# Routing of a mixture-of-experts layer: integer indices compared as they are, picks seen kept per row group, slots summed straight into the records

## The chip, the core and the metric

The kernel runs on one core of one Trainium2 chip, in one launch. The time is device microseconds (us) of that core; three runs of the kernel before took 697.89, 700.32 and 699.39 us, median 699.39. The engines named below are TensorE (PE; its weight loads are PEld), VectorE (DVE), ScalarE (ACT), GpSimd (POOL) and SyncE (SP, which here only issues DMAs).

## The reference, cut to what matters

Tokens are rows of x, 2 x 2048 of them, 256 wide. An RWKV attention layer with a layer norm gives x1; then eight experts with top-2 routing and a second layer norm follow.

```python
x = layernorm(x + attention(x))                 # k, v, r projections, WKV scan over time, Wo
logits = einsum('bsd,de->bse', x, Wg) + bg      # 8 experts
scores, idx = top_k(logits, 2); scores = softmax(scores)
comb = (one_hot(idx, 8) * scores[..., None]).sum(axis=1)
h = einsum('td,edf->etf', tokens, W1) + b1      # 256 -> 1024, per expert
a = where(even expert, gelu(h), silu(h))
y = einsum('etf,efd->etd', a, W2) + b2          # 1024 -> 256
x = layernorm(x + einsum('te,etd->td', comb, y))
```

## The kernel before, in words

The work has two phases. Phase A goes over time in NCH = 8 chunks of TC = 256 steps of both batches, so that a chunk has N = 512 tokens, held as J = 4 row groups of P = 128 tokens (one token to a partition). Phase B goes over blocks of BLK = 256 tokens of one expert each, some 35 of them.

Every engine has its own program, and the order within it is written out by hand; semaphores tie them together. In phase A each engine works through steps i, and one step holds pieces of several chunks: on VectorE, step i is `stabilise(i)` (scan over k, tiles `o_all`, `nd`), `divide(i-1)` (tile `newton`), `place(i-3)`, `accumulate(i)` (the two long scans `q_all`, `p_all`), `numerator(i)`, the residual and the statistics of i-1, `choose(i-2)`, and `lower_halves(i+2)` (tile `xl`, the low part of the transposed input of a later chunk, for which ScalarE first makes `xh`). In the last steps chunk 5 is placed at the end of step 7, and chunks 6 and 7 are chosen and placed one after the other.

The routing of a chunk c is in these pieces:

- `score_rows` (TensorE) puts the 4 x 8 logits of each token into `lg_ps`.
- `choose` (VectorE) takes the maxima `m8` and their indices `i8` (uint32), casts the indices to float (`idxf`, L1265), compares them with 0..7 into the one-hot `hot` [4 groups, 2 picks, 8 experts] (L1267), and adds the two picks into `picks` (bf16, L1270). Semaphore `route` counts each of these.
- `rank_picks` (TensorE) works out how many tokens ahead of each one, in earlier partitions, earlier row groups and earlier chunks, chose each expert: five matmuls of at most 32 columns into `rank_ps`; the last (L803) multiplies `seen`, the sum over earlier chunks per partition and expert, [128, 8].
- `place` (VectorE) makes the softmax weights (L1329 to L1334), then `rank` (adds the start of each expert's region in DRAM, L1342), `newly` (picks of this chunk, summed over the row groups, L1343), `spread` (`hot` times `rank`, L1345), `seen` += `newly` (L1347), `slot_f` (sum of `spread` over experts, L1349), its integer copy `slot_i` (L1351) and its copy into the record (L1352). Semaphore `slots` counts them, and most of them wait for the one before.
- `send_records` (POOL) waits for all seven counts and then issues eight indirect DMAs, which scatter the chunk's 261-number records (x1, token number, two slots, two weights) into the expert regions (`records_dram`, L614). After them POOL computes the mean and spread of the next chunk (`spread_of`, tiles `var_e` to `shift`), from which ScalarE normalises x1.

Phase B's start hangs on the routing's end. SP loads two blocks early (`recs`), once chunks 0 to 4 (those below KNOWN = 5) are scattered; the scatter of chunk 5 waits for that load. After the last chunk is ranked, TensorE waits for `seen` (the fourth count of `slots`), counts all picks with one matmul (L859), and then begins the first expert product `hT_ps` (L871). VectorE makes the table of blocks from the counts. `idle_products` (L680) are matmuls whose result nobody reads.

Of the kernel before, what the change touches and what calls it, by code (L numbers as in the profile page):

```python
# [23 lines left out]
ALU = mybir.AluOpType  # L24
# [8 lines left out]
P = 128  # L33
# [50 lines left out]
def build(nc, x, decay, first, mix_k, mix_v, mix_r, wkT, wvT, wrT, woT, w1, b1, w2, b2, wgT, bg, out):  # L84
# [40 lines left out]
    with ExitStack() as ctx:  # L125
        def sb(name, shape, dt=F32, where=ctx):
            return where.enter_context(nc.sbuf_tensor(name, shape, dt))
# [78 lines left out]
        odds = sb("odds", [P, J], F32, phase_a)  # L206
        both = sb("both", [P, J], F32, phase_a)
        i8 = sb("i8", [P, J, 8], U32, phase_a)
        idxf = sb("idxf", [P, J, 2], F32, phase_a)
        hot = sb("hot", [P, J, 2, E], F32, phase_a)  # L210
        seen = sb("seen", [P, E], BF16, phase_a)
        newly = sb("newly", [P, E], F32, phase_a)
        picks = sb("picks", [P, J, E], BF16, phase_a)
        rank = sb("rank", [P, J, E], F32, phase_a)
        spread = sb("spread", [P, J, 2, E], F32, phase_a)
        slot_f = sb("slot_f", [P, J, 2], F32, phase_a)
        slot_i = [sb(f"slot_i{n}", [P, J * 2], I32, phase_a) for n in range(RECS)]
        const_rows = sb("const_rows", [5 * CC, P], F32, phase_a)
        b1_rows = sb("b1_rows", [E * FC, P], F32, phase_a)
# [100 lines left out]
        c_bn, c_mv, c_var, c_rstd, c_res = (sem(n) for n in ("c_bn", "c_mv", "c_var", "c_rstd", "c_res"))  # L320

        REC_DMAS = 2 * J * 16
        ROUTE1, ROUTE2 = 2 * J + 3, 7

        def chunks(body):

# [347 lines left out]
        def _(pe):  # L674
# [107 lines left out]
            def turn_early(n):  # L782
# [7 lines left out]
                        ins = pe.transpose(xT2_ps[:, cc, h * P:(h + 1) * P], recs[n][:, h, cc * P:(cc + 1) * P], ident[:])  # L790
                ins.then_inc(tx_done, 1)

            def rank_picks(c):
                if c.number == 0:
                    pe.wait_ge(halves_made, 1)
                pe.wait_ge(route, c.upto(ROUTE1))
                if c.number == KNOWN:
                    pe.matmul(early_ps, ones_h[:], seen[:], start=True, stop=True).then_inc(known, 1)
                pe.matmul(rank_ps, before_h[:], picks[:], start=True, stop=False)
                for j in range(J - 1):  # L800
                    pe.matmul(rank_ps[:, j + 1:J, :], ones_h[:], picks[:, j:j + 1, :].broadcast_to([P, J - 1 - j, E]),
                              start=False, stop=False)
                pe.matmul(rank_ps, ones_h[:], seen[:].unsqueeze(1).broadcast_to([P, J, E]), start=False, stop=True).then_inc(rank_done, 1)  # L803

            def step(i):
                if i.number == -2:
# [9 lines left out]
                else:  # L816
# [38 lines left out]
                    if routed.exists:  # L855
                        rank_picks(routed)
                        if routed.number == NCH - 1:
                            pe.wait_ge(slots, routed.upto(ROUTE2, 4))
                            pe.matmul(cnt_ps, ones_h[:], seen[:], start=True, stop=True).then_inc(cnt_done, 1)  # L859

            chunks(step)

# [274 lines left out]
        def _(dve):  # L1137
# [114 lines left out]
            def choose(c):  # L1252

                dve.wait_ge(lg_done, c.upto(1))
                take_wait(dve)
                for j in range(J):
                    dve.max(m8[:, j, :], lg_ps[:, j, :]).then_inc(route, 1)
                dve.wait_ge(route, c.upto(ROUTE1, J))
                take_wait(dve)
                for j in range(J):  # L1260
                    dve.max_index(i8[:, j, :], m8[:, j, :], lg_ps[:, j, :]).then_inc(route, 1)
                after(dve, weighed, (c - 1).upto(1))
                dve.tensor_tensor(gap[:], m8[:, :, 1], m8[:, :, 0], ALU.subtract).then_inc(gap_done, 1)
                dve.wait_ge(route, c.upto(ROUTE1, 2 * J))
                dve.tensor_copy(idxf[:], i8[:, :, 0:2]).then_inc(route, 1)  # L1265
                dve.wait_ge(route, c.upto(ROUTE1, 1 + 2 * J))
                dve.tensor_tensor(hot[:], expert_no[:].unsqueeze(1).unsqueeze(1).broadcast_to([P, J, 2, E]),  # L1267
                                  idxf[:].unsqueeze(3).broadcast_to([P, J, 2, E]), ALU.is_equal).then_inc(route, 1)
                dve.wait_ge(route, c.upto(ROUTE1, 2 + 2 * J))
                dve.tensor_tensor(picks[:], hot[:, :, 0, :], hot[:, :, 1, :], ALU.add).then_inc(route, 1)  # L1270

            def accumulate(i):
# [52 lines left out]
            def place(c):  # L1325
# [14 lines left out]
                    dve.wait_ge(known, 2)  # L1340
                    dve.tensor_tensor(rest_no[:], region_no[:], done_f[:], ALU.add).then_inc(known, 1)
                dve.tensor_tensor(rank[:], rank_ps, region_no[:].unsqueeze(1).broadcast_to([P, J, E]), ALU.add).then_inc(slots, 1)  # L1342
                dve.tensor_reduce(newly[:], picks[:].rearrange("p j e -> p e j"), AX.X, ALU.add).then_inc(slots, 1)  # L1343
                dve.wait_ge(slots, c.upto(ROUTE2, 2))
                dve.tensor_tensor(spread[:], hot[:], rank[:].unsqueeze(2).broadcast_to([P, J, 2, E]), ALU.mult).then_inc(slots, 1)  # L1345
                dve.wait_ge(slots, c.upto(ROUTE2, 3))
                dve.tensor_tensor(seen[:], seen[:], newly[:], ALU.add).then_inc(slots, 1)  # L1347
                dve.wait_ge(slots, c.upto(ROUTE2, 4))
                dve.tensor_reduce(slot_f[:], spread[:], AX.X, ALU.add).then_inc(slots, 1)  # L1349
                dve.wait_ge(slots, c.upto(ROUTE2, 5))  # L1350
                dve.tensor_copy(slot_i[c.number % RECS][:].rearrange("p (j k) -> p j k", j=J), slot_f[:]).then_inc(slots, 1)  # L1351
                dve.tensor_copy(rec[c.number % RECS][:, :, C + 1:C + 3], slot_f[:]).then_inc(slots, 1)  # L1352

            def residual_0(c):
                add_residual(c, 0)
# [153 lines left out]
```

## Time and profile before

| | |
|---|---|
| median of three runs | 699.39 us |
| the profiled execution | 698.79 us, its span 696.8 us |
| PE busy | 630.9 us, 91% |
| DVE busy | 464.1 us, 67%, 1075 instructions |
| ACT busy | 377.9 us, 54% |
| POOL busy | 333.2 us, 48% |
| mean granted TensorE clock | 0.952 |

The shares are means over both phases. In phase B, from 300 us on, PE is busy all the time and DVE a little over half of it; in phase A the two are close to each other, as the rows below show. A span starts with the first instruction and ends with the last; the profiled execution took 1.99 us more than its span.

### The profile page before, as it was taken

How to read it: one execution, taken by the hardware profiler on the slowest of the kernel's cores; microseconds unless marked ns; L12 is line 12 of the kernel's file. 1: busy time of each engine (PE TensorE's matmuls, PEld its weight loads, DVE VectorE, ACT ScalarE, POOL GpSimd, SP SyncE). 2: the span in 40 equal slices, each digit the busy share in tenths (PEclk: the TensorE clock that was granted, in tenths of full speed). 3: DMA queues.
4: the chain of work that ended last, by engine and by line, in shares of the span. 5: the costliest groups of instructions: out<-in, count | busy, mean ns of one | idle time of the engine just before them, and what ended most of it. 6: DMA issues, size and time to landing. Idle time of an engine off the chain costs nothing.

```text
span 696.8 us, 14651 instructions
## 1 busy us (share of the span) xinstructions
PE 630.9 (91%) x4525; PEld 581.3 (83%) x4525; DVE 464.1 (67%) x1075; ACT 377.9 (54%) x690; POOL 333.2 (48%) x322
## 2 busy tenths in 40 slices
PE   8999999999977788999999999999999999999800
PEld 5787887878854578999999999999999999999700
DVE  4879999999998566556556565565565465545334
ACT  3566686585764133645464646466464646464317
POOL 6111037536546768239356384356394275222325
PEclk9999999999989779999999999999999999999955
DMA  8500222321324745532534425325317313231376
GB/s 254 157 32 0 91 91 70 132 83 55 107 86 154 232 148 151 162 60 63 144 48 146 71 42 160 60 49 144 72 24 183 47 42 47 48 48 15 36 226 276
DMA packets 53309, 70.61 MB, mean 101 GB/s; under 512 B 5482, under 2 KB 46900, under 8 KB 53076
## 3 DMA queue, kind: packets, MB, share of 16 engines
q1 hardware_dynamic: 31012, 43.24, 18.8%
q0 software_dynamic: 13216, 17.09, 13.4%
q10 hardware_dynamic: 8976, 8.82, 4.5%
q8 instruction: 73, 1.20, 0.7%
q14 instruction: 32, 0.26, 0.1%
HBM read 40.86 MB, written 29.06 MB: 100 GB/s over the span
## 4 chain that ended last, share of the span: by engine, by line
PE 64%; DVE 16%; issue 8%; ACT 4%; DMA 3%; POOL 2%; SPq 0%; DVEq 0%; ACTq 0%; POOLq 0%
PE hT_ps L871 27%; PE y_ps L880 26%; PE vr_ps L708 3%; PE k_ps L708 2%; PE xT_ps L889 2%; ACT zz L1133 2%; DVE o_all L1221 2%; POOL records_dram L614 2%; DMA zz<-x_dram 1%; DVE newton L1244 1%; DVE newton L1249 1%; DVE stats L1319 1%; DVE newton L1242 1%; DMA recs<-records_dram 1%; DVE num L1311 1%
## 5 line engine op out<-in xcount | busy, mean ns | idle before, releaser
L871 PE MATMUL hT_ps<-xTh,wx 128*128 128x256 f32 x1120 | 207.5, 283 | 2.6 <-DVE aTl L1191 1.3
L652 POOL DMA_INDIRECT x_dram<-y_sb,dest x70 | 108.5, 1550 | 195.3 <-DVE y_sb L1208 128.1
L880 PE MATMUL y_ps<-wx,aTh 128*128 128x256 f32 x1088 | 191.1, 279 | 3.0 <-DVE y_sb L1208 3.0
L871 PEld LDWEIGHTS hT_ps<-xTh,wx 128*128 128x128 f32 x1120 | 174.8, 189 | 3.3 <-DVE aTl L1191 2.4
L1191 DVE TENSOR_TENSOR aTl<-hT_ps,aTh 128x512 fp32r<-128x512 f32 x140 | 93.3, 688 | 121.7 <-ACT aTh L1094 121.7
L880 PEld LDWEIGHTS y_ps<-wx,aTh 128*128 128x128 f32 x1088 | 165.5, 189 | 3.4 <-issue 3.4
L871 PE MATMUL hT_ps<-xTl,wx 128*128 128x256 f32 x560 | 156.9, 280 | 0.0
L880 PE MATMUL y_ps<-wx,aTl 128*128 128x256 f32 x544 | 151.7, 279 | 0.0
L1088 ACT ACT_TABLE_LOAD x33 | 42.3, 1283 | 162.5 <-PE hT_ps L871 160.8
L1088 ACT ACTIVATE hT_ps<-hT_ps,b_c 128x256 f32<-128x256 f32 x280 | 113.5, 468 | 22.8 <-PE hT_ps L871 21.2
L614 POOL DMA_INDIRECT records_dram<-rec,slot_i x64 | 76.7, 1198 | 67.6 <-DVE rec L1352 35.9
L871 PEld LDWEIGHTS hT_ps<-xTl,wx 128*128 128x128 f32 x560 | 106.1, 189 | 0.0
L880 PEld LDWEIGHTS y_ps<-wx,aTl 128*128 128x128 f32 x544 | 102.2, 188 | 0.0
L708 PE MATMUL vr_ps<-xh,wq 128*128 128x512 f32 x256 | 86.7, 411 | 0.0
L1094 ACT ACTIVATE aTh<-hT_ps 128x512 fp32r<-128x512 f32 x140 | 84.3, 649 | 0.0
L558 POOL TENSOR_TENSOR wx<-staging,wx 128x512 fp32r<-128x512 f32 x56 | 70.3, 1293 | 0.6
L708 PEld LDWEIGHTS vr_ps<-xh,wq 128*128 128x128 f32 x256 | 49.7, 194 | 11.8 <-ACT v L975 0.3
L1206 DVE TENSOR_TENSOR y_ps<-y_ps,b_b 128x256 f32<-128x256 f32 x70 | 30.1, 430 | 43.9 <-DVE weight L1187 18.9
L708 PE MATMUL vr_ps<-xl,wq 128*128 128x512 f32 x128 | 51.9, 405 | 0.0
L708 PE MATMUL k_ps<-xh,wq 128*128 128x512 f32 x128 | 42.2, 401 | 5.2 <-DVE nd L1228 4.2
L1208 DVE TENSOR_SCALAR y_sb<-y_ps,weight 128x256 f32<-128x256 f32 x70 | 33.9, 484 | 2.5
L708 PEld LDWEIGHTS k_ps<-xh,wq 128*128 128x128 f32 x128 | 24.2, 189 | 11.9 <-issue 6.3
(203 smaller groups left out, 853.5 us busy)
## 6 DMA issues: line engine op xcount, KB each, us to landing
staging<-in_L_ffn_W SPq DMA_DIRECT2D x16, 1024.0 KB
recs<-records_dram ACTq DMA_DIRECT2D x33, 261.0 KB, 3.0
xin<-in_L_attn_x SPq DMA_DIRECT2D x16, 256.0 KB, 4.3
xres<-in_L_attn_x SPq DMA_DIRECT2D x16, 256.0 KB, 3.1
x_dram<-rec SPq DMA_DIRECT2D x16, 256.0 KB, 3.4
zz<-x_dram SPq DMA_DIRECT2D x8, 512.0 KB, 9.2
out<-zz SPq DMA_DIRECT2D x8, 512.0 KB, 3.5
records_dram<-pad_rec SPq DMA_DIRECT2D x8, 261.0 KB, 2.9
```

What stands on the lines that cost most here:

```text
L558: pool.tensor_tensor(wx[:, e % 2, 1, at], raw[:, at], wx[:, e % 2, 0, at].bitcast(F32), ALU.subtract).then_inc(weights_ready if n == LOWER ...
L614: pool.indirect_dma_start(xs, bass.IndirectOffsetOnAxis(ap=slot_i[at][:, n:n + 1], axis=0), rec[at][:, j, :], None, bounds_check=DUMMY - 1 ...
L652: pool.indirect_dma_start(sums, bass.IndirectOffsetOnAxis(ap=dest[t.slot][:, h:h + 1], axis=0), y_sb[t.slot][:, h, :], None, bounds_check= ...
L708: ins = pe.matmul(out_ps.rearrange("p (b t) -> p b t", b=B), wq[:, mat, now, part, cc, oc * P:(oc + 1) * P], xpart[c.slot][:, cc, :, now:n ...
L871: ins = pe.matmul(hT_ps[b][:, f, :], wx[:, s, part, off:off + P], xpart[t.slot % 2][:, cc, :], start=k == 0, stop=k == len(terms) - 1)
L880: ins = pe.matmul(y_ps[h], apart[t.slot % 2][:, fc, h * P:(h + 1) * P], wx[:, s, part, off:off + C], start=k == 0, stop=k == len(terms) - 1)
L889: ins = pe.transpose(xT2_ps[:, cc, h * P:(h + 1) * P], recs[u.slot][:, h, cc * P:(cc + 1) * P], ident[:])
L1088: act.activation(hT_ps[b][:, f, :], hT_ps[b][:, f, :], func, bias=b1_c[:, bass.ds(expert * FC + (2 * b + f), 1)]).then_inc(act_done, 1)
L1094: act.activation(aTh[u.slot % 2][:, 2 * b - 2:2 * b, :], hT_ps[b - 1][:], ACT.Copy).then_inc(aTh_done, 1)
L1191: dve.tensor_tensor(aTl[u.slot % 2][:, 2 * b:2 * b + 2, :], hT_ps[b][:], aTh[u.slot % 2][:, 2 * b:2 * b + 2, :].bitcast(F32), ALU.subtract ...
L1206: dve.tensor_tensor(y_ps[h], y_ps[h], b2_b[:, bass.ds(expert * C, C)], ALU.add).then_inc(bias_added, 1)
L1208: dve.tensor_scalar(y_sb[u.slot][:, h, :], y_ps[h], weight[u.slot][:, h:h + 1], None, ALU.mult).then_inc(y_done, 1)
```

## The change

Three buffers go (`idxf`, `newly`, `slot_f`). `hot` compares the uint32 indices directly. `seen` has one row per row group, [128, 4, 8], so that the picks are added to it elementwise, with no sum over the groups; TensorE does that sum, with four matmuls into the same accumulator where there was one. The slots are summed straight into the record, and `slot_i` is cast from there.

```diff
-        seen = sb("seen", [P, E], BF16, phase_a)
+        seen = sb("seen", [P, J, E], BF16, phase_a)
-        ROUTE1, ROUTE2 = 2 * J + 3, 7
+        ROUTE1, ROUTE2 = 2 * J + 2, 5
 # TensorE
+            def count(out_ps):
+                for j in range(J):
+                    ins = pe.matmul(out_ps, ones_h[:], seen[:, j, :], start=j == 0, stop=j == J - 1)
+                return ins
 # rank_picks
-                pe.matmul(rank_ps, ones_h[:], seen[:].unsqueeze(1).broadcast_to([P, J, E]), start=False, stop=True).then_inc(rank_done, 1)
+                for j in range(J):
+                    ins = pe.matmul(rank_ps, ones_h[:], seen[:, j:j + 1, :].broadcast_to([P, J, E]), start=False, stop=j == J - 1)
+                ins.then_inc(rank_done, 1)
 # after the last chunk (and for chunk KNOWN, into early_ps, in the same way)
-                            pe.wait_ge(slots, routed.upto(ROUTE2, 4))
-                            pe.matmul(cnt_ps, ones_h[:], seen[:], start=True, stop=True).then_inc(cnt_done, 1)
+                            pe.wait_ge(slots, routed.upto(ROUTE2, 2))
+                            count(cnt_ps).then_inc(cnt_done, 1)
 # VectorE, choose
-                dve.tensor_copy(idxf[:], i8[:, :, 0:2]).then_inc(route, 1)
-                dve.wait_ge(route, c.upto(ROUTE1, 1 + 2 * J))
                 dve.tensor_tensor(hot[:], expert_no[:].unsqueeze(1).unsqueeze(1).broadcast_to([P, J, 2, E]),
-                                  idxf[:].unsqueeze(3).broadcast_to([P, J, 2, E]), ALU.is_equal).then_inc(route, 1)
+                                  i8[:, :, 0:2].unsqueeze(3).broadcast_to([P, J, 2, E]), ALU.is_equal).then_inc(route, 1)
 # VectorE, place
                 dve.tensor_tensor(rank[:], rank_ps, region_no[:].unsqueeze(1).broadcast_to([P, J, E]), ALU.add).then_inc(slots, 1)
-                dve.tensor_reduce(newly[:], picks[:].rearrange("p j e -> p e j"), AX.X, ALU.add).then_inc(slots, 1)
-                dve.wait_ge(slots, c.upto(ROUTE2, 2))
+                dve.tensor_tensor(seen[:], seen[:], picks[:], ALU.add).then_inc(slots, 1)
+                dve.wait_ge(slots, c.upto(ROUTE2, 1))
                 dve.tensor_tensor(spread[:], hot[:], rank[:].unsqueeze(2).broadcast_to([P, J, 2, E]), ALU.mult).then_inc(slots, 1)
                 dve.wait_ge(slots, c.upto(ROUTE2, 3))
-                dve.tensor_tensor(seen[:], seen[:], newly[:], ALU.add).then_inc(slots, 1)
+                dve.tensor_reduce(rec[at][:, :, C + 1:C + 3], spread[:], AX.X, ALU.add).then_inc(slots, 1)
                 dve.wait_ge(slots, c.upto(ROUTE2, 4))
-                dve.tensor_reduce(slot_f[:], spread[:], AX.X, ALU.add).then_inc(slots, 1)
-                dve.wait_ge(slots, c.upto(ROUTE2, 5))
-                dve.tensor_copy(slot_i[c.number % RECS][:].rearrange("p (j k) -> p j k", j=J), slot_f[:]).then_inc(slots, 1)
-                dve.tensor_copy(rec[c.number % RECS][:, :, C + 1:C + 3], slot_f[:]).then_inc(slots, 1)
+                dve.tensor_copy(slot_i[at][:].rearrange("p (j k) -> p j k", j=J), rec[at][:, :, C + 1:C + 3]).then_inc(slots, 1)
```

On VectorE, in the first step that places a chunk, these rows stand before, from the last product of `divide` to the first copy of `accumulate` (the three rows between are the softmax weights):

```order
L1249 SCALAR_TENSOR_TENSOR newton<-newton,num 128x2x256 x2
L1329 TENSOR_SCALAR both<-odds 128x4
L1332 RECIPROCAL rec<-both 128x4
L1334 TENSOR_TENSOR rec<-odds,rec 128x4
L1342 TENSOR_TENSOR rank<-small_ps,region_no 128x32
L1343 TENSOR_REDUCE newly<-picks 128x8
L1345 TENSOR_TENSOR spread<-hot,rank 128x64
L1347 TENSOR_TENSOR seen<-seen,newly 128x8
L1349 TENSOR_REDUCE slot_f<-spread 128x8
L1351 CAST slot_i<-slot_f 128x8
L1352 COPY rec<-slot_f 128x4x2
L1279 COPY B<-q_all 128x4
```

And now, on the same engine at the same place:

```order
L1253 SCALAR_TENSOR_TENSOR newton<-newton,num 128x2x256 x2
L1331 TENSOR_SCALAR both<-odds 128x4
L1334 RECIPROCAL rec<-both 128x4
L1336 TENSOR_TENSOR rec<-odds,rec 128x4
L1344 TENSOR_TENSOR rank<-small_ps,region_no 128x32
L1345 TENSOR_TENSOR seen<-seen,picks 128x32
L1347 TENSOR_TENSOR spread<-hot,rank 128x64
L1349 TENSOR_REDUCE rec<-spread 128x4x2
L1351 CAST slot_i<-rec 128x8
L1281 COPY B<-q_all 128x4
```

Seven rows behind the weights have become five: the sum over row groups and the copy into the record are gone, and `seen`, with 32 elements instead of 8, stands ahead of `spread`.

On TensorE these rows stand before at the end of phase A, from the last idle products to the first expert product:

```order
L680 MATMUL k_ps<-ones_h 128x512 x6
L799 MATMUL small_ps<-picks,before_h 128x32
L801 MATMUL small_ps<-picks,ones_h 128x24
L801 MATMUL small_ps<-picks,ones_h 128x16
L801 MATMUL small_ps<-picks,ones_h 128x8
L803 MATMUL small_ps<-seen,ones_h 128x32
L859 MATMUL small_ps<-seen,ones_h 128x8
L871 MATMUL hT_ps<-xTh,wx 128x256
```

And now:

```order
L677 MATMUL k_ps<-ones_h 128x512 x6
L801 MATMUL small_ps<-picks,before_h 128x32
L803 MATMUL small_ps<-picks,ones_h 128x24
L803 MATMUL small_ps<-picks,ones_h 128x16
L803 MATMUL small_ps<-picks,ones_h 128x8
L806 MATMUL small_ps<-seen,ones_h 128x32 x4
L792 MATMUL small_ps<-seen,ones_h 128x8 x4
L875 MATMUL hT_ps<-xTh,wx 128x256
```

The matmuls on `seen` are four where there was one, in the ranking and in the count; nothing else on TensorE has another place.

## Rows read from the trace of the kernel before

**Rows 1.** Windows: stretch, its length, busy us (x instructions) per engine, PEclk, DMA.
```profile
120.00:150.00 30.00, 27.75 (x140) 22.86 (x141) 29.16 (x64) 21.18 (x32) 13.91 (x16) 1.00 0.35 116
166.00:168.00 2.00, 2.00 (x8) 1.71 (x7) 1.68 (x20) 1.31 (x4) 1.54 (x4) 0.50 0.19 67
250.00:254.00 4.00, 4.00 (x19) 4.00 (x20) 3.56 (x16) 0.81 (x2) 2.15 (x3) 0.51 0.32 104
```
**Rows 2.** Timeline of PE: start, us, line, operation, count, idle before it and releaser.
```profile
145.24 0.22 PE L801 MATMUL small_ps<-picks,ones_h 128*128 128x24 bf16 x3
145.32 0.18 PE L803 MATMUL small_ps<-seen,ones_h 128*128 128x32 bf16 x1
146.96 0.47 PE L708 MATMUL k_ps<-xh,wq 128*128 128x512 f32 x1 [1.47 <-DVE nd L1228]
```
**Rows 3.** Chain that ended last, in order of time: start, us, what.
```profile
201.08 1.29 DVE newton L1249 x2
...
219.66 3.20 DMA recs<-records_dram
...
234.47 1.05 POOL rstd L591
...
249.97 9.08 PE hT_ps L871 x60
```
**Rows 4.** Timeline of DVE, `choose` in the step from 120 us.
```profile
141.46 0.17 DVE L1265 CAST idxf<-i 128x8 f32<-128x8 uint32 x1
141.67 0.23 DVE L1267 TENSOR_TENSOR hot<-expert_no,idxf 128x64 f32<-128x64 f32 x1
141.93 0.19 DVE L1270 TENSOR_TENSOR picks<-hot 128x32 bf16<-128x32 f32 x1
```
**Rows 5.** Timeline of DVE, `place` in the same step.
```profile
125.43 0.18 DVE L1342 TENSOR_TENSOR rank<-small_ps,region_no 128x32 f32<-128x32 f32 x1
125.53 0.20 DVE L1343 TENSOR_REDUCE newly<-picks 128x8 f32<-128x32 bf16 x1
125.76 0.22 DVE L1345 TENSOR_TENSOR spread<-hot,rank 128x64 f32<-128x64 f32 x1
126.02 0.17 DVE L1347 TENSOR_TENSOR seen<-seen,newly 128x8 bf16<-128x8 bf16 x1
126.22 0.22 DVE L1349 TENSOR_REDUCE slot_f<-spread 128x8 f32<-128x64 f32 x1
126.47 0.17 DVE L1351 CAST slot_i<-slot_f 128x8 int32<-128x8 f32 x1
126.56 0.16 DVE L1352 COPY rec<-slot_f 128x8 f32<-128x8 f32 x1
126.63 0.16 DVE L1279 COPY B<-q_all 128x4 f32<-128x4 f32 x1
```
**Rows 6.** Timeline of DVE: first row of `lower_halves` in two steps.
```profile
89.65 0.17 DVE L1296 CAST xl<-xl 128x4 fp32r<-128x4 f32 x1
...
168.24 0.17 DVE L1296 CAST xl<-xl 128x4 fp32r<-128x4 f32 x1
```
**Rows 7.** Timeline of ACT: the `xh` for which those rows wait.
```profile
88.54 1.07 ACT L1019 ACTIVATE xh<-xT_ps 128x512 fp32r<-128x512 f32 x2
...
166.81 1.07 ACT L1019 ACTIVATE xh<-xT_ps 128x512 fp32r<-128x512 f32 x2
```
**Rows 8.** Timeline of POOL: last scatter of chunk 3 and what follows it.
```profile
191.53 0.97 POOL L614 DMA_INDIRECT records_dram<-rec,slot_i  x1 [0.30 <-issue]
192.88 0.20 POOL L588 TENSOR_TENSOR var_e<-mv,eps_b 128x4 f32<-128x4 f32 x1 [0.38 <-issue]
```
**Rows 9.** Timeline of DVE: the last chunk's `place`.
```profile
248.94 0.19 DVE L1342 TENSOR_TENSOR rank<-small_ps,region_no 128x32 f32<-128x32 f32 x1 [0.57 <-PE small_ps L803]
...
249.54 0.17 DVE L1347 TENSOR_TENSOR seen<-seen,newly 128x8 bf16<-128x8 bf16 x1
```
**Rows 10.** Timeline of PE: the count of all picks, ahead of the first expert product.
```profile
249.76 0.19 PE L859 MATMUL small_ps<-seen,ones_h 128*128 128x8 bf16 x1 [1.36 <-DVE seen L1347]
```

More of the change, by code:

```diff
@@ L208, in build @@
         i8 = sb("i8", [P, J, 8], U32, phase_a)
-        idxf = sb("idxf", [P, J, 2], F32, phase_a)
         hot = sb("hot", [P, J, 2, E], F32, phase_a)
-        seen = sb("seen", [P, E], BF16, phase_a)
-        newly = sb("newly", [P, E], F32, phase_a)
+        seen = sb("seen", [P, J, E], BF16, phase_a)
         picks = sb("picks", [P, J, E], BF16, phase_a)
@@ L215, in build @@
         spread = sb("spread", [P, J, 2, E], F32, phase_a)
-        slot_f = sb("slot_f", [P, J, 2], F32, phase_a)
         slot_i = [sb(f"slot_i{n}", [P, J * 2], I32, phase_a) for n in range(RECS)]
@@ L797, in rank_picks @@
                 if c.number == KNOWN:
-                    pe.matmul(early_ps, ones_h[:], seen[:], start=True, stop=True).then_inc(known, 1)
+                    count(early_ps).then_inc(known, 1)
                 pe.matmul(rank_ps, before_h[:], picks[:], start=True, stop=False)
@@ L1264, in choose @@
                 dve.wait_ge(route, c.upto(ROUTE1, 2 * J))
-                dve.tensor_copy(idxf[:], i8[:, :, 0:2]).then_inc(route, 1)
+                dve.tensor_tensor(hot[:], expert_no[:].unsqueeze(1).unsqueeze(1).broadcast_to([P, J, 2, E]),
+                                  i8[:, :, 0:2].unsqueeze(3).broadcast_to([P, J, 2, E]), ALU.is_equal).then_inc(route, 1)
                 dve.wait_ge(route, c.upto(ROUTE1, 1 + 2 * J))
-                dve.tensor_tensor(hot[:], expert_no[:].unsqueeze(1).unsqueeze(1).broadcast_to([P, J, 2, E]),
-                                  idxf[:].unsqueeze(3).broadcast_to([P, J, 2, E]), ALU.is_equal).then_inc(route, 1)
-                dve.wait_ge(route, c.upto(ROUTE1, 2 + 2 * J))
                 dve.tensor_tensor(picks[:], hot[:, :, 0, :], hot[:, :, 1, :], ALU.add).then_inc(route, 1)
```

## The prediction, made before the changed kernel had run

> **What bounds the kernel now.** I read the windows first, in stretches of 30 us, to see which engine is full in which stage, then the chain of waits in order of time, then the timelines of the engines at the places that the change touches. In the windows the reader is to see that phase A is VectorE's: from 120 to 150 us VectorE is busy for 29.16 of 30 us at the full TensorE clock, and TensorE for 27.75 [rows 1]. The timeline shows that the rest of VectorE's time is the 0.03 us between an instruction and one that waits for its result, not a wait for another engine, and that TensorE in the same step waits 1.47 us for VectorE's `nd` [rows 2]. So from about 60 to 204 us the length of a step, 26.2 us, is the sum of VectorE's instructions and of the small steps between dependent ones.
>
> The chain confirms it and says where VectorE stops being the bound. It is on VectorE up to `newton` at 201.08 us, where `place` of chunk 4 follows; then it goes to POOL, which scatters chunk 4, to the early load of `recs` at 219.66, back to POOL, which may scatter chunk 5 only after that load and computes the last chunk's spread at 234.47, and over ScalarE and TensorE to the first expert product at 249.97 [rows 3]. From there it is TensorE to 660 us, and a tail. Nothing behind 250 us is changed, and I take it to move as a whole.
>
> **The change part by part.** *The cast of the indices.* It starts at 141.46 and `hot` at 141.67 [rows 4]. Both wait for the indices only, so `hot` will stand where the cast stood: 0.21 us less in each `choose`. Reading integers costs nothing that the trace can see: the cast reads uint32 in 0.17 us, the copies between floats beside it take 0.16 [rows 4, 5]. An integer operand inside a comparison isn't shown anywhere; its bounds are nothing and one cast's step, 0.21 us, which would take back all of this term. I take nothing, since the same engine reads the same tile at the same price.
>
> *`place`.* From the start of `rank` to the first copy of `accumulate` it takes 126.63 - 125.43 = 1.20 us [rows 5]. After the change I build it from the same rows. `seen` waits for nothing and is issued 0.10 us behind `rank`, as `newly` was. `spread` waits for `rank` alone, which ends after 0.18 us, and 0.03 us is the step to a waiting instruction (`newly` ends at 125.73, `spread` starts at 125.76): 0.22. The reduce waits for `spread`; the instruction that waits for it now starts 0.26 after it: 0.48. The cast of the slots starts 0.25 after the reduce: 0.73. The next independent instruction follows 0.08 later: 0.81. So each `place` is 0.39 us shorter, although `seen` grows from 8 to 32 elements: it takes about what `picks` takes, 0.19 instead of 0.17 [rows 4, 5], and it lies under the wait for `rank`. Writing the sums into the record, 8 numbers with a stride, isn't shown; the copy that did it took 0.16 us, no more than one without a stride. Bounds of the whole of `place`: 0.25 us, if only the issue steps of independent instructions fall away, and 0.45.
>
> *TensorE.* Three matmuls more for each ranking. The three of L801 take 0.08 us from start to start [rows 2], so 0.08 us per chunk. They lie in front of TensorE's wait for `nd`, of 1.47 us [rows 2]; VectorE's gain of 0.60 per step shortens that wait to about 0.8, so it still covers them. If it didn't, eight chunks would cost 0.6 us.
>
> *What is late next.* Where a step of VectorE shrinks by 0.6 us, whatever it waits for with less slack than that stops it. The tightest is `lower_halves`, which waits for ScalarE's `xh`. In the step of chunk 0's choice `xh` ends at 88.54 + 1.07 = 89.61 and VectorE goes on at 89.65: no slack, so the cast of chunk 0 brings nothing. In the step at 168 us `xh` ends at 167.88 and VectorE needs it at 168.24, a slack of 0.36 [rows 6, 7]; there TensorE ran at half clock (0.50 from 166 to 168 us [rows 1]), which made the transposes late. Since `nd` let TensorE go, VectorE will have gained 0.39 + 0.21 = 0.60, so 0.24 is lost. In the other two steps the slack is about 1 us. POOL ends the scatter of chunk 3 at 192.50 and starts the next spread at 192.88 [rows 8], a close race, but both sides of it count from the end of `place`, so it doesn't change.
>
> *Sum up to 204 us.* The `place` of chunks 0 to 4 lie on VectorE's path: 5 x 0.39 = 1.95. The `choose` of chunks 1 to 4: 4 x 0.21 = 0.84. Less 0.24 at 168 us: 2.55 us. The choices and placings of chunks 5 and 6 are hidden: POOL waits for the load of `recs` and its own eight scatters meanwhile.
>
> *The end of phase A.* The last `rank` starts at 248.94 and `seen` ends at 249.71, TensorE counts at 249.76 and begins the products at 249.97 [rows 3, 9, 10]. Now `seen` ends 0.29 after `rank` starts, not 0.77: 0.48 earlier. Against it stand three more matmuls in the last ranking and three in the count, here at half clock, which I put at 0.1 each time. The choice's 0.21 is hidden by idle products ahead of the ranking. So 0.28 us. Total: 2.8 us.
>
> The Trainium skill has a rule that speaks against this size. In "VectorE: DVE Perf Modes", in the section on the TRN2 errata, a VectorE operation from SBUF costs 58 cycles of 0.96 GHz plus its elements; by it the three small operations are worth an estimated 0.21 us a chunk (three of 69 to 94 ns, less 25 ns for the longer `seen`). It counts no wait between dependent instructions; the trace disagrees, with 0.20 to 0.26 us between such starts [rows 4, 5]. By the page's price the whole would be some 1.1 us.
>
> Against the profiled execution this is 698.79 - 2.8 = 696.0 us. That execution lies 0.6 us below the median of the runs, 699.39, from which the same gain gives 696.6; I predict 696.4.
>
> **The rivals.** *Only issue steps go.* If dependent instructions wait on something that stays (the semaphore counts, say), each operation removed is worth the step between independent ones, 0.07 to 0.10 us (`slot_i` to `rec` to `B`, `rank` to `newly` [rows 5]), 0.25 a chunk. Five chunks give 1.2 us: 698.0. The rows of dependent starts speak against it. The page's rule above ends at about the same time.
>
> *TensorE or ScalarE takes over.* If half clock falls into two or three of the five steps, not one, each costs 0.24 to 0.6 us of the gain, and with the added matmuls about 1.3 us is left: 697.9. For it: a step of TensorE has only 1.47 us to spare, and the low clock at 166 us used that up. Against it: in the steps before, the clock was full.
>
> *The clock comes back later (slower).* The first products start at half clock, 0.50 from 250 to 254 us [rows 1], and TensorE is the bound from there on. If the low clock lasts through the whole first product group, which took 9.08 us from 249.97 [rows 3], its other 5 us take 10, and the kernel ends at 696.4 + 5 = 701.4. It decides once the loss is larger than the 2.8 us won. For it: TensorE's idle time at this place changes (the wait of 1.36 us for `seen` shrinks [rows 10]), and the clock fell more than once here. Against it: a shorter idle time should help, if anything. The Trainium skill ("TensorE: Matmul & The Clock Gate", Part 1) calls the window over which the clock is judged free-running, so that no place in the program is safe from it; no run here shows that yet.
>
> *More than counted.* If the clock rises as much earlier, or the low clock at 166 us moves to where TensorE has slack, up to 1.7 us come on top: 694.7.
>
> **How the numbers follow.** What a measurement of this kernel can tell from no change is about 0.3%, 2.1 us. My forecast has 0.57, the first rival 0.14, the second 0.14, the slower one 0.07, the gain above count 0.08. Of the forecast's 0.57 a tenth falls short of 2.1 us by the scatter of runs (697.89 to 700.32): faster 0.51 + 0.08 and a little of the second rival, 0.61; slower, the third and scatter, 0.08; the same, 0.31. The range of the likeliest alone is 695.4 to 697.3; for 8 in 10 it reaches up to the two smaller gains with half the scatter, 699.0, and down to 694.5.
>
> **What would show it.** On VectorE, `rank` to the first copy of `accumulate` 0.81 us instead of 1.20, `hot` at once behind the indices, a step of 25.6 us where it was 26.2; `hot` with integers about 0.23 us, `seen` 0.19; `xl` with a wait of 0.2 us for `xh` in the step with low clock; TensorE's wait for `nd` near 0.8 us; the first expert product near 247.2 us. I would be wrong if `hot` took 0.4 us, if steps shrank by 0.25 only, or if the first product came 2.8 us earlier and the end didn't.

## The result, and the profile after

The changed kernel took 696.0 us (median of 6 runs, 694.94 to 697.47), the kernel before in the same comparison 699.49 (6 runs): a ratio of 0.9945, interval 0.9922 to 0.9968, so 2.2 to 5.5 us less than before's 699.5 (the interval is one of 95%). Two more comparisons gave 0.9949 (0.9926 to 0.9973) and 0.994 (0.9919 to 0.9961). The forecast was 696.4, from a gain of 2.8 us. The profiled execution of the changed kernel has a span of 693.0 us, 3.8 less than before's 696.8; and where these 3.8 lie is not where I had put them, as shown below.

The page of the changed kernel, part 1, engine by engine (busy us, share, instructions):

```profile
PE 629.8 (91%) x4555; PEld 581.2 (84%) x4555; DVE 459.1 (66%) x1051; ACT 378.3 (55%) x690; POOL 334.1 (48%) x322
```

VectorE has 24 instructions fewer, three for each of eight chunks, and 5.0 us less busy time (464.1 before).

The timeline of VectorE after, `choose` and then `lower_halves` in the step from 120 us, which answers to [rows 4] (start, us, line, operation, idle before it):

```profile
140.88 0.15 DVE L1267 TENSOR_TENSOR gap<-m 128x4 f32<-128x4 f32 x1
141.00 0.23 DVE L1269 TENSOR_TENSOR hot<-expert_no,i 128x64 f32<-128x64 f32 x1
141.26 0.19 DVE L1272 TENSOR_TENSOR picks<-hot 128x32 bf16<-128x32 f32 x1
141.74 0.17 DVE L1298 CAST xl<-xl 128x4 fp32r<-128x4 f32 x1 [0.29 <-ACT xh L1023]
```

`hot` stands where the cast stood, 0.12 us behind the start of `gap`, and takes 0.23 us with an integer operand, as it did with a float. But VectorE then waits 0.29 us for `xh`, in a step in which it hadn't waited before.

The chain of work that ended last, as the page sums it up, of before and then of after (share of the span by engine), says the same:

```profile
PE 64%; DVE 16%; issue 8%; ACT 4%; DMA 3%; POOL 2%; SPq 0%; DVEq 0%; ACTq 0%; POOLq 0%
```

```profile
PE 71%; DVE 11%; issue 6%; ACT 5%; DMA 3%; POOL 2%; SPq 0%; DVEq 0%; ACTq 0%; POOLq 0%
```

In the step from 120 us the chain of before runs over VectorE all the way. That of after runs over TensorE and comes back to VectorE at `xl`, by way of ScalarE's `xh`:

```profile
129.59 5.63 PE vr_ps L705 x24
...
137.27 1.88 PE small_ps L727 x16
139.15 1.35 PE xT_ps L696 x8
...
140.64 1.08 ACT xh L1023 x2
```

VectorE's timeline again, `place` in that step, which answers to [rows 5]:

```profile
125.33 0.18 DVE L1344 TENSOR_TENSOR rank<-small_ps,region_no 128x32 f32<-128x32 f32 x1
125.43 0.17 DVE L1345 TENSOR_TENSOR seen<-seen,picks 128x32 bf16<-128x32 bf16 x1
125.55 0.22 DVE L1347 TENSOR_TENSOR spread<-hot,rank 128x64 f32<-128x64 f32 x1
125.80 0.22 DVE L1349 TENSOR_REDUCE rec<-spread 128x8 f32<-128x64 f32 x1
126.06 0.17 DVE L1351 CAST slot_i<-rec 128x8 int32<-128x8 f32 x1
126.14 0.17 DVE L1281 COPY B<-q_all 128x4 f32<-128x4 f32 x1
```

From `rank` to the next copy it is 126.14 - 125.33 = 0.81 us, the forecast to the hundredth, and every row stands within 0.02 us of where the working put it. For the four other chunks up to chunk 4 it is 0.81 or 0.82 us as well.

The chain of waits after, which answers to [rows 3] (start, us, what):

```profile
199.97 1.29 DVE newton L1253 x2
...
218.09 3.02 DMA recs<-records_dram
...
233.17 1.05 POOL rstd L588
...
267.95 3.98 DMA recs<-records_dram
```

Read against [rows 3], and with the small shift that the setup brings (VectorE's first `newton` starts at 47.34 us, before at 47.11), the places are 1.34, 1.80 and 1.53 us earlier than before. TensorE's timeline at the end of phase A answers to [rows 10]:

```profile
247.89 0.27 PE L792 MATMUL small_ps<-seen,ones_h 128*128 128x8 bf16 x4 [1.12 <-DVE seen L1345]
248.11 0.55 PE L875 MATMUL hT_ps<-xTh,wx 128*128 128x256 f32 x1
```

The last `rank` starts at 247.56 and the product at 248.11, 0.55 us later, where it was 249.97 - 248.94 = 1.03. So the first product comes 1.86 us earlier, and I had expected 2.8.

These 1.86 us also hold two things that the change doesn't touch and that nearly cancel. The last chunk's scores, on TensorE, and the first `MAX8` of its choice, on VectorE, of before and then of after:

```profile
242.12 3.58 PE L730 MATMUL small_ps<-wg,x1T 128*128 128x8 f32 x16
245.84 0.39 DVE L1257 MAX8 m<-small_ps 128x8 f32<-128x8 f32 x4 [2.89 <-issue]
```

```profile
240.65 1.95 PE L727 MATMUL small_ps<-wg,x1T 128*128 128x8 f32 x16
244.66 0.39 DVE L1261 MAX8 m<-small_ps 128x8 f32<-128x8 f32 x4 [3.10 <-remote]
```

Before, the scores ran at half clock (0.50 from 240 to 248 us) and took 3.58 us; after, the clock was back (0.91 from 240 to 242, then 1.00) and they took 1.95. But then VectorE began 2.06 us behind their end, where before it was 0.14, and the profile doesn't say what for.

A few microseconds on, nothing is left of it. This is TensorE's timeline of before and then of after, at the transposes of the first block whose records it has to wait for:

```profile
272.17 0.63 PE L889 MATMUL xT_ps<-ident,recs 128*128 128x128 f32 x4 [0.76 <-DMA recs<-records_dram]
```

```profile
272.17 0.63 PE L893 MATMUL xT_ps<-ident,recs 128*128 128x128 f32 x4 [0.95 <-DMA recs<-records_dram]
```

The windows say why. Before and then after (columns as in [rows 1]):

```profile
248.00:252.00 4.00, 2.62 (x16) 2.39 (x15) 2.98 (x18) 0.65 (x1) 0.77 (x1) 0.50 0.11 38
252.00:256.00 4.00, 4.00 (x29) 4.00 (x28) 2.55 (x7) 1.96 (x5) 3.08 (x4) 0.76 0.69 236
```

```profile
248.00:252.00 4.00, 4.00 (x22) 3.99 (x22) 3.49 (x17) 0.81 (x2) 1.97 (x2) 0.50 0.25 85
252.00:256.00 4.00, 4.00 (x28) 4.00 (x27) 1.92 (x4) 2.06 (x6) 3.22 (x3) 0.75 0.56 184
```

The clock comes back at the same time in both (0.76 and 0.75 of full from 252 to 256 us). The products that began earlier began in the half-clock stretch: by 252 us 18 matmuls of the product had begun, where before 10 had (the counts above include the small ones of ranking and count). So the head start is worth about half. TensorE then waits longer for `aTl` (2.25 us at 262.48, before 1.32 at 262.76), and the load of the records, issued 0.32 us earlier, took 0.33 us longer.

The end of the chain of before, and then of after, has the remaining difference:

```profile
654.55 5.93 PE y_ps L880 x48
...
667.82 7.57 DMA zz<-x_dram
```

```profile
653.32 5.74 PE y_ps L884 x48
...
665.63 3.65 DMA zz<-x_dram
```

The last product starts 1.23 us earlier; from it to the end it is 42.25 us before and 39.7 after. The first load of the final layer norm took 3.65 us, not 7.57, and the work behind that load took 2.3 us longer. That is no work of the change: in the second profiled executions of the two kernels the same load took 6.85 (before) and 7.41 us (changed), and the whole tail 40.7 and 41.0.

### The profile page after: what moved, and what is told of

Same layout as the page of the kernel before. It is cut to its first block, busy times and chain, and to the rows that moved or that the text cites. A ratio compares the mean times of both kernels' runs of the same rounds, so it can differ in the third digit from the quotient of the medians.

```text
span 693.0 us, 14687 instructions
## 1 busy us (share of the span) xinstructions
PE 629.8 (91%) x4555; PEld 581.2 (84%) x4555; DVE 459.1 (66%) x1051; ACT 378.3 (55%) x690; POOL 334.1 (48%) x322
## 4 chain that ended last, share of the span: by engine, by line
PE 71%; DVE 11%; issue 6%; ACT 5%; DMA 3%; POOL 2%; SPq 0%; DVEq 0%; ACTq 0%; POOLq 0%
PE y_ps L884 27%; PE hT_ps L875 26%; PE vr_ps L705 6%; PE k_ps L705 5%; ACT zz L1137 2%; PE xT_ps L893 2%; PE wo_ps L713 2%; DVE o_all L1225 2%; POOL records_dram L611 2%; PE small_ps L727 1%; DMA recs<-records_dram 1%; DVE xl L1301 1%; PE xT_ps L775 1%; PE xT_ps L696 1%; DVE nd L1232 1%
```

## Experiments

The kernels below ran in three groups of four, each group on one chip with the kernel before beside it. The chips differ (the kernel before took 698.93, 694.84 and 695.9 us in the three groups), so times are compared by the ratio to the kernel before in the same group. Stages of one execution are compared by the profile.

**The two kernels again.** No edit.

> The kernel before, unchanged, to see how stages vary by themselves. My theory: phase A is fixed by VectorE and the same to 0.3 us (first rank near 99.2 us, last slot of chunk 4 near 204.2, first expert product near 250.0); what varies between executions is where TensorE's clock falls and the tail after the last y product (42.3 us in the first trace, 39.7 in that of the changed kernel). Median 699.3, span about 697. Rival, that the 3.8 us between the two profiled spans are all the change: the tail is 42 us again.

> The changed kernel, unchanged, the same question. My theory: place 0.82 us, first rank to the end of chunk 4's slots about 103.2 us (before: 104.9), first product near 248.1; of the 1.9 us won there, 0.6 to 1.2 are left from 300 us on, and the rest of any difference in span is the tail. Median 696.0 to 697.0. Rival, that the gain arises in phase B as well: the start of the last y product (653.3 in the first trace, 654.6 before) is again over 1 us earlier, while the first product isn't.

Before again: ratio 1.0023 (0.9997 to 1.0048), span 698.6. So the kernel before came out 1.6 us apart from itself, with an interval that just takes in no difference. After again: 0.9949, span 696.0. My expectation that phase A of the kernel before is the same to 0.3 us was wrong: chunk 4's slots ended at 205.18 us, not 204.07, and the first product began at 251.33. VectorE's timeline in this run has the cause:

```profile
116.91 0.18 DVE L1296 CAST xl<-xl 128x4 fp32r<-128x4 f32 x1 [1.05 <-ACT xh L1016]
```

and the windows what stands ahead of it:

```profile
88.00:92.00 4.00, 4.00 (x13) 3.13 (x12) 3.74 (x19) 3.73 (x6) 2.39 (x6) 0.57 0.00 0
114.00:118.00 4.00, 4.00 (x20) 3.28 (x19) 2.73 (x19) 2.28 (x5) 3.41 (x6) 1.00 0.28 100
```

TensorE ran at half clock for most of 88 to 92 us, where the first execution had none, got behind, and made VectorE wait 1.05 us for `xh` a step later: that step is 27.44 us instead of 26.2. So where the half clock falls moves one and the same kernel by a microsecond.

In the changed kernel, from the first `newton` to the end of chunk 4's slots it is 155.31 and 155.20 us in these two executions (155.25 in a third, below), against 156.96 and 158.26 before. That is 1.65 us at the least, where I had 2.55.

**The cast alone, and all but the cast.**

```diff
 # cast_only: on the kernel before
-                dve.tensor_copy(idxf[:], i8[:, :, 0:2]).then_inc(route, 1)
-                dve.wait_ge(route, c.upto(ROUTE1, 1 + 2 * J))
-                                  idxf[:].unsqueeze(3)...
+                                  i8[:, :, 0:2].unsqueeze(3)...
 # place_only: on the changed kernel, the same lines put back
# (both with the counts of the semaphore route to match)
```

> The kernel before without the cast of the indices; all else as before. My theory: hot directly behind the indices, 0.20 us less per choose; choices of chunks 1 to 4 lie on VectorE's path: slots of chunk 4 end 0.8 us earlier, first product 0.8 earlier, in the end 0.3 to 0.8: about 698.8. Rival (an integer operand costs as much as the cast): hot takes 0.4 us and nothing is won, 699.4. Rival (only issue steps): 0.1 us per choose, 699.1.

> The changed kernel with the cast of the indices put back; place is the changed one. My theory: place 0.82 us instead of 1.20, five of them on the path: slots of chunk 4 end 1.9 us earlier than before, less waits for xh, which should be shorter than in the changed kernel (0 to 0.1 us each, not 0.3), since each step gains 0.38 and not 0.59; about 697.3. Rival (only issue steps go): 0.15 us per place, 698.7.

The cast alone: 0.9999 (0.9979 to 1.0019), and all but the cast: 0.9951 (0.9929 to 0.9973). VectorE's timeline in cast_only:

```profile
141.83 0.14 DVE L1263 TENSOR_TENSOR gap<-m 128x4 f32<-128x4 f32 x1
141.95 0.23 DVE L1265 TENSOR_TENSOR hot<-expert_no,i 128x64 f32<-128x64 f32 x1
```

The cast's 0.2 us is saved in place: the steps of this run are 26.22, 26.00 and 25.99 us, and up to chunk 4's slots it is 156.38 us, 0.58 less than before's 156.96. But it is worth nothing that the runs can tell; 0.8 us, as I expected, lies inside the interval, which allows a gain of 1.5 us at most. As far as the runs can tell, the change's whole gain can be had with the cast kept. In place_only's own trace, half clock near 90 us made one step 27.05 us, so its stages tell less than its runs.

**Waits, or operations?** The kernel before with all its operations:

```diff
-                dve.wait_ge(slots, c.upto(ROUTE2, 2))
+                dve.wait_ge(slots, c.upto(ROUTE2, 1))
                 dve.tensor_tensor(spread[:], ...).then_inc(slots, 1)
-                dve.wait_ge(slots, c.upto(ROUTE2, 3))
+                dve.wait_ge(slots, c.upto(ROUTE2, 2))
                 dve.tensor_tensor(seen[:], seen[:], newly[:], ALU.add).then_inc(slots, 1)
-                dve.wait_ge(slots, c.upto(ROUTE2, 4))
+                dve.wait_ge(slots, c.upto(ROUTE2, 3))
                 dve.tensor_reduce(slot_f[:], ...).then_inc(slots, 1)
```

> The kernel before with every operation kept and only two waits of place moved: spread waits for rank alone (not for newly), slot_f waits for spread alone (not for seen), so that seen slips under the wait for spread. My theory (the waits between dependent operations are what counts): rank to the next copy takes 0.89 to 0.98 us instead of 1.20, 60 to 80% of the changed kernel's 0.39, and slots of chunk 4 end about 1.2 us earlier: about 698. Rival (operations removed count, each with its fixed cost): place 1.17 us or more, nothing won, 699.3.

Ratio 0.9969 (0.9949 to 0.9989). VectorE's timeline in this run:

```profile
126.16 0.18 DVE L1342 TENSOR_TENSOR rank<-small_ps,region_no 128x32 f32<-128x32 f32 x1
126.26 0.20 DVE L1343 TENSOR_REDUCE newly<-picks 128x8 f32<-128x32 bf16 x1
126.38 0.22 DVE L1345 TENSOR_TENSOR spread<-hot,rank 128x64 f32<-128x64 f32 x1
126.52 0.16 DVE L1347 TENSOR_TENSOR seen<-seen,newly 128x8 bf16<-128x8 bf16 x1
126.63 0.22 DVE L1349 TENSOR_REDUCE slot_f<-spread 128x8 f32<-128x64 f32 x1
126.89 0.17 DVE L1351 CAST slot_i<-slot_f 128x8 int32<-128x8 f32 x1
126.97 0.17 DVE L1352 COPY rec<-slot_f 128x8 f32<-128x8 f32 x1
127.04 0.17 DVE L1279 COPY B<-q_all 128x4 f32<-128x4 f32 x1
```

Seven operations take 0.88 us instead of 1.20, so 0.31 to 0.32 of the changed kernel's 0.39 come from three waits that ask for one count less: `spread` no longer waits for `newly`, nor the sum for `seen`, and `seen` slips in under the wait for `spread`. An operation that stands under another's wait costs next to nothing; one that nothing hides, like the copy into the record, costs its 0.07 to 0.08. This rules out the rival that only issue steps go. In time it is 2.2 us of the 3.5, with intervals that overlap.

**Does TensorE eat the rest?** The changed kernel, with half of `v`'s products left out from chunk 2 on:

```diff
+                if mat == 1 and c.number > 1:
+                    terms = terms[:6]
```

> The changed kernel with three quarters... half of v's projection left out for chunks 2 and on (12 of 24 matmuls less, 2.8 us of TensorE per step; the values of v are then not the reference's, and the blocks of phase B may be others, so only phase A counts). Theory that TensorE ate the missing part of the gain: steps of VectorE (newton to newton) are 25.6 us, not 25.85 to 25.98, and no wait for xh is left, wherever the clock is low. Rival that something on VectorE itself is longer: steps stay at 25.9.

The steps that the other kernels have at 25.6 to 26.2 us are 25.57, 26.64 and 25.60 us here, and VectorE never waits for `xh`. Two of them are the 25.6 I had predicted. The third has a wait of a new kind, for `wo_ps` (0.74 us), and so have the steps ahead of the three and behind them: 27.45 us where the changed kernel has 25.15 (a wait of 2.75), and 26.22 where it has 24.39 (a wait of 1.75). Windows and TensorE's timeline of this run:

```profile
140.00:146.00 6.00, 6.00 (x33) 5.22 (x34) 5.48 (x29) 3.21 (x5) 3.08 (x6) 0.72 0.14 47
```

```profile
122.27 0.77 PE L707 MATMUL k_ps<-xh,wq 128*128 128x512 f32 x1 [1.92 <-DVE nd L1234]
```

So the expectation holds in part: VectorE itself is as short as worked out, and no step is 25.9 by itself. But taking work off TensorE didn't help: from the first `newton` to chunk 4's slots it is 159.44 us in this trace, 4.1 more than in the changed kernel. TensorE waited 1.6 to 3.8 us for `nd` where the changed kernel's waits are 0.96 at most, and the mean granted clock over the 8 runs of this kernel was 0.941 (0.935 to 0.944), against 0.952 (0.948 to 0.957) over the 23 of the kernel before on the same chip.

**More idle work, three ways.** On the changed kernel:

```diff
 # steady3
+                    if 2 <= i.number <= 5:
+                        pe.wait_ge(res_done, (i - 2).upto(2))
+                        idle_products(3, wo_ps...)
                     if ahead.exists:
                         project_k(ahead)
 # idle4; idle2 has 2 in place of 4
                         if routed.number == NCH - 1:
+                            idle_products(4, k_ps[:, 1, :])
                             pe.wait_ge(slots, routed.upto(ROUTE2, 2))
```

> The changed kernel with three idle matmuls (0.65 us at full clock) ahead of project_k in steps 2 to 5, where TensorE waits for nd. Theory that low clock in the steps comes from TensorE's idle moments: no half clock before the last chunk, steps of 25.6 us, 1 us less. Rival that TensorE has no room to give: in steps in which it is behind the three matmuls cost 0.65 us each; steps of 26 us or more, 1 to 2 us more than the changed kernel (0.997 to 0.998 of before).

> The changed kernel with four idle matmuls of 512 columns ahead of TensorE's last count, in its wait of 1.1 us for seen. Theory: in the changed kernel TensorE was at half clock until 255 to 265 us by the trace's span, whether its first product began at 248 or 250 us, so that the products' beginning is not worth its full time; more work in front of it brings the full clock back earlier: first product to the load of block 2's records 22 us instead of 24, time 1 to 2 us less, about 695. Rival: the low clock depends on TensorE's idle time earlier (216 to 238 us) and stays: the four matmuls take 0.9 us at half clock, all but 0.1 in the wait, 696.3.

> The changed kernel with two idle matmuls ahead of the last count, where four took 0.7 us too long (they ran at half clock, 0.42 us each) though the full clock was back early. Theory: they fit the wait of 1.1 us, so the first product begins no later than in the changed kernel; if they also bring the clock back early as four did, first product to block 2's records is 21.5 us and the time 2 us below the changed kernel (0.992 of before). Rival: where the clock stands there is chance, and the four matmuls' early full clock was luck: 24 us again and 0.995.

> The changed kernel once more, as the measure for the three beside it on this chip. Expected: 0.995 of the kernel before, as in both comparisons so far; steps of VectorE 25.6 us where TensorE is at full clock all along, 25.8 to 26.0 where it isn't; first product to the load of block 2's records near 24 us.

steady3: 0.9963 (0.9941 to 0.9984), not better than the changed kernel beside it, 0.994. In its trace, which is of the fastest of its 12 runs, two steps are 25.57 and 25.59 us and the one between them is 26.51, with a wait of 0.60 us for `wo_ps`. It has one stretch of half clock up to 198 us (at 113 us), where the three traces of the changed kernel have two or three; it didn't prevent them all, and the runs show no gain. idle4: 0.9935 (0.9913 to 0.9957); its four products, at half clock, held up the first expert product, 1.61 us behind the last `rank` where the changed kernel has 0.55. idle2: 0.9912 (0.9886 to 0.9938), with the changed kernel beside it at 0.994 (0.9919 to 0.9961). The windows at the first products, of idle4, of idle2, and of the changed kernel in the third group:

```profile
248.00:252.00 4.00, 4.00 (x30) 3.45 (x29) 2.66 (x13) 0.81 (x2) 2.21 (x3) 0.80 0.13 44
```

```profile
248.00:252.00 4.00, 4.00 (x32) 4.00 (x32) 3.52 (x15) 1.49 (x4) 2.61 (x3) 0.88 0.39 132
```

```profile
248.00:252.00 4.00, 4.00 (x32) 4.00 (x31) 2.02 (x5) 2.56 (x8) 3.09 (x4) 0.86 0.70 235
```

With idle products the clock is back early (0.80 and 0.88 against 0.50 in the first execution of the changed kernel), and from the first product to block 2's records it is 21.3 and 20.7 us instead of 24.1. The third window looks as if the changed kernel could do that by itself (0.86), but its first product had begun at 244.70 us, over 3 us earlier than the others. Counted from the first product, the full clock is back after 0.7 us in idle4, 1.3 in idle2 and 1.2 in woven (below), the three with idle products; in the 11 other traces it takes 3.3 to 6.1 us, but for steady3, where it was full already. So an effect of the idle products on the clock is likely. What it brings in time isn't: the runs put idle2 ahead by 1.4 us of mean (690.7 over 6 runs, 692.1 over 8), with intervals that overlap: unclear.

Why the third execution of the changed kernel is so early at the first product (197.71 us from the first `newton`, 200.77 and 200.67 in the two others) shows at the last chunk's choice: VectorE's `MAX8` stands 0.14 us behind the scores, not 2.06 or 1.52, and `rank` 0.24 us behind the last ranking matmul, not 0.79 or 1.45. No trace says what these waits are for. All traces of the second and third group have at most 0.38 us of the two together; those of the first group have 0.98 to 2.97, and the first pair 0.67 (before) and 2.85 (after).

**A woven order.** For chunks 0 to 4, `place` with the weights' operations between those of the rank, on the changed kernel; woven has idle2's two products as well.

```diff
                 dve.tensor_scalar(both[:], odds[:], 1.0, None, ALU.add).then_inc(scored, 1)
+                # rank; reciprocal; spread (waits for rank); second weight; seen
                 dve.tensor_reduce(rec[at][:, :, C + 1:C + 3], spread[:], AX.X, ALU.add).then_inc(slots, 1)
```

> The changed kernel with the weights' three operations and the rank's chain woven together for chunks 0 to 4 (both, rank, reciprocal, spread, second weight, seen, reduce, cast); no operation added or removed. By the steps between dependent operations (0.20 to 0.26 us) both to the next copy takes 0.92 us instead of 1.31. Theory that VectorE alone sets the step: steps 0.39 shorter, 1.9 us less, 694.4. Rival that TensorE has little left to give (it already makes VectorE wait 0.3 us for xh in two steps of the changed kernel): of 1.9 us some 0.5 to 1 are left, 695.6, and the waits for xh grow to 0.5 or more.

> The woven order of place for chunks 0 to 4 together with two idle matmuls ahead of the last count, as the version that might beat both. Theory: both gains are small and add up in part: 0.993 of before. Rival: neither brings anything beyond the changed kernel: 0.995.

interleave: 0.9946 (0.9926 to 0.9965). Its `both` starts at 124.81 and the next copy at 125.73, 0.92 us as worked out, where the changed kernel took 1.31. The steps are 25.95, 25.77 and 25.71 us, not 25.2, and the waits for TensorE have grown: 0.48 and 0.49 for `xh`, 0.46 and 0.67 for `wo_ps`. The rival that TensorE has little left is right, and it had promised 0.5 to 1 us; even that doesn't show in the runs. woven: 0.991 (0.9881 to 0.9939), the lowest ratio of all, but not apart from idle2 (0.9912), so nothing says that the weaving adds to it. Both lie clear of the kernel before, neither is shown to beat the changed one.

## Why the prediction was right, and where it wasn't

The time was right: 696.4 predicted, 696.0 measured, and 2.8 us less predicted against a gain of some 3.5 with an interval from 2.2. That the two lie so close is in part luck: the terms of the sum that the traces let one read come to 2.1 us (1.65 up to chunk 4's slots, 0.48 behind the last `rank`), and where the rest of the runs' gain lies isn't known. Step by step:

- *What bounds phase A.* Right for the kernel before. Shortening VectorE's step moved everything up to the first product, but in the changed kernel the chain runs for the most part over TensorE from 94.8 us to the `xh` at 166.6 us, and comes back to VectorE only between `xl` and `nd`: there VectorE no longer sets the pace alone.
- *The cast.* Right in place (0.20 to 0.21 us, `hot` 0.23 with integers), wrong in worth: of 0.84 us for chunks 1 to 4 the runs of cast_only show nothing, and its interval allows 1.5 at most.
- *`place`.* Right: 0.81 or 0.82 us in every chunk, and waits_only shows why: for the most part (0.31 to 0.32 of 0.39) it is waits, not the number of operations. The estimate by the page "VectorE: DVE Perf Modes" of the Trainium skill (its section on the TRN2 errata), 0.21 us a chunk for all three operations, was too low here: the trace has 0.20 for the cast and 0.39 for `place`.
- *What is late next.* This term of the sum was mis-sized. I took 0.24 us for one wait for `xh`, in the step at 168 us, and it was 0.29 there. But the changed kernel's trace has another of 0.29 us, at 141.74, and one of 0.30 before the scans at 117.23, whose release the profile puts on VectorE itself and which I haven't tracked down; it was in cast_only's trace too. Together they are 0.88 us. A stretch of half clock that the first execution of before didn't have fell at 114 to 118 us:

```profile
114.00:118.00 4.00, 4.00 (x12) 3.13 (x11) 3.52 (x21) 3.97 (x6) 3.53 (x7) 0.57 0.28 100
120.00:150.00 30.00, 29.25 (x157) 23.94 (x156) 28.97 (x61) 20.88 (x32) 13.92 (x16) 1.00 0.33 107
```

  The slack of 1 us that I had read for the step at 142 us counts from a TensorE that waits for `nd`. Held up at 114 to 118 us, it didn't wait at 121 us but went on at once, and `xh` came late. TensorE is now busy for 29.25 of 30 us where it was 27.75 [rows 1]: it is nearly the bound. Steps of the changed kernel were 25.85, 25.98 and 25.98, not 25.6. Up to chunk 4's slots 1.65 us were won, not 2.55; without any wait I had 2.79, the three waits leave 1.91, and the other 0.26 stay open. So a rival to which I had given 0.14, that TensorE takes over when half clock falls into two steps or more, came true in its mechanism, inside my likeliest case.
- *TensorE's added matmuls.* L806, four of them, began and were done within 0.25 us; they are a part of the 0.9 us that is missing at most (0.08 a step), and weren't tried by themselves.
- *The end of phase A.* From the last `rank` to the product 0.38 us expected (0.48 for `seen` less 0.1 for the count), 0.48 measured, in both pairs of executions: `seen` comes as early as worked out, and the four counting matmuls took 0.27 us together, in which their greater number doesn't show. What the working left out is larger: TensorE's clock at the scores and the waits of VectorE behind them, up to 3 us.
- *Nothing behind 250 us changes, and it moves as a whole.* This step failed. In the one pair of traces the head start of 1.86 us was gone at 272.17, with the clock back at the same time in both, 0.6 us were there from 300 us on, 1.23 at the last product, and 2.6 us came from a shorter tail. From the first product to the end it was 446.8 and 447.3 us in the two executions before, and 444.9, 448.5 and 444.5 in three of the changed kernel. The spread of that stage is as large as the gain.
- *The slower rival*, half clock through the whole first product group, wasn't seen in any of the runs of this kernel. Idle matmuls ahead of it may help (idle2); that stays unclear.

What stays open: whether the 3.5 us of the runs hold more than the roughly 2 us that phase A's traces show (202.86 and 204.41 us from the first `newton` to the first product before, 200.77 and 200.67 after). The executions before differ among each other by 1.6 us there, so that these four allow 2.1 to 3.7 us in phase A alone; the third of the changed kernel, on another chip without a trace of before beside it, has 197.71. No experiment here separates this from luck in phase B.

## What to carry to other kernels

On an engine that is the bound, look at which small operations wait for which: here, with 8 to 64 elements a partition, an independent one cost 0.07 to 0.10 us, a dependent one 0.20 to 0.26, and moving waits was worth nearly as much as all of the change to `place` (0.31 to 0.32 of 0.39 us). Before counting the same saving for every repetition, check how far the next engine is behind: with TensorE at 27.75 of 30 us, a step shrank by the full 0.6 us only where TensorE had not been held up by a stretch of half clock, and the second small saving brought nothing that the runs show. A gain of 3 us in a kernel whose executions spread over more than that is shown by ratios of many runs; a single pair of spans put 2.6 of 3.8 us where the change had no part.

## What the runs showed of the hardware that I hadn't expected

Where TensorE's half clock falls in the loop differs between executions of one kernel (near 165 and 193 us in the first of the kernel before, near 90, 167 and 201 us in the second), though TensorE was busy almost without a break, and one such stretch in the wrong step costs 1.24 us (27.44 instead of 26.20). The Trainium skill ("TensorE: Matmul & The Clock Gate", Part 1) calls the window free-running; these runs agree with that so far as the place changes from run to run.

The step changes, but not the place within it. In 13 of the 14 traces (all but light_pe), each stretch that begins between 84 and 198 us begins within 1.2 us of the end of a step's 16 score matmuls (`small_ps` from `wg`, 8 columns each), where the transposes of the next input follow: at 114.0, with the scores ended at 113.0, and at 165.2, ended at 164.8, in the changed kernel's trace. No run moved or removed these matmuls, so that they bring the low clock isn't shown. Behind 198 us, where TensorE is idle more often, stretches begin at other places too.

TensorE with less work (light_pe) had the lower granted clock, 0.941 against 0.952 in the mean of runs on one chip, and phase A took longer, not shorter.
